# A layer-norm variance computed from its parts and a tile list cut in two, in a single-core attention and mixture-of-experts kernel

## The reference

```python
x = x + _layernorm(attention_block(_layernorm(x), ...))      # heads, two inner layer norms, a small feed-forward
x_flat = _layernorm(x).reshape(-1, 128)                      # 4096 rows
router_probs = softmax(x_flat @ gate_w)                      # 8 experts
expert_idx, expert_w = argmax and its probability
for e in range(8):
    y = gelu(x_flat @ w1[e] + b1[e], approximate=False) @ w2[e] + b2[e]     # 128 -> 512 -> 128
    out = out + where(expert_idx == e, expert_w, 0)[:, None] * y
x = x + _layernorm(out)
```

## Time and profile before

| what | value |
|---|---|
| median of 3 runs | 532.84 us (529.25, 532.84, 534.83) |
| the profiled execution's own time | 529.64 us |
| its span | 527.8 us |
| busy PE / DVE / ACT / POOL | 371.3 / 401.3 / 352.7 / 260.5 us |
| mean granted TensorE clock | 0.875 of 2.4 GHz |

### The profile page before, as it was taken

How to read it: one execution, slowest core, us unless ns; L and a number is a source line. 1 busy time by engine, 2 the same in 40 slices (tenths; PEclk the granted TensorE clock), 3 DMA queues, 4 the chain that set the end, 5 groups by cost and what they waited for, 6 DMA issues and landing times.

```text
span 527.8 us, 8507 instructions
## 1 busy us (share of the span) xinstructions
PE 371.3 (70%) x2412; PEld 255.7 (48%) x2412; DVE 401.3 (76%) x877; ACT 352.7 (67%) x730; POOL 260.5 (49%) x399
## 2 busy tenths in 40 slices
PE   0858688887777878887787889773000499999960
PEld 0744356554444444544444433663000388888840
DVE  4987658899999999999999973588783037667670
ACT  0234434888988888889888794788440387777730
POOL 8365015544444445545333103673667027777774
PEclk9999956788999899889999889976555699999995
DMA  9561211455555465545545199990111217776600
GB/s 208 41 145 36 57 31 41 103 141 126 129 141 133 110 140 121 126 115 141 143 121 127 38 125 151 132 239 21 42 36 57 74 51 193 217 194 177 172 15 0
DMA packets 81244, 58.18 MB, mean 110 GB/s; under 512 B 17619, under 2 KB 72919, under 8 KB 81196
## 3 DMA queue, kind: packets, MB, share of 16 engines
q1 hardware_dynamic: 75142, 53.12, 45.6%
q0 software_dynamic: 2496, 4.29, 2.4%
q10 hardware_dynamic: 3558, 0.20, 0.5%
HBM read 35.38 MB, written 23.11 MB: 111 GB/s over the span
## 4 chain that ended last, share of the span: by engine, by line
DVE 35%; PE 33%; POOL 8%; issue 8%; ACT 7%; DMA 6%; ACTq 1%; SPq 1%; POOLq 0%; DVEq 0%
DVE mxs L1753 10%; DVE big L1802 7%; PE ps L1593 7%; DVE big L1837 7%; PE ps L1604 6%; POOL sorted_rows L783 4%; DVE gb L1667 2%; PE ps L1265 2%; DMA qk_parts<-proj 2%; PE ps L1223 1%; PE ps L1537 1%; DMA arena<-m_parts 1%; PE ps L1396 1%; PE ps L1383 1%; PE ps L1538 1%
## 5 line engine op out<-in xcount | busy, mean ns | idle before, releaser
L1837 DVE SCALAR_TENSOR_TENSOR big<-big,ps 128x1024 f32<-128x1024 f32 x64 | 76.6, 1214 | 7.1 <-PE ps L1396 6.7
L1753 DVE TENSOR_REDUCE mxs<-ps 128x4 f32<-128x1024 f32 x64 | 76.6, 1217 | 2.4 <-PE ps L1265 1.2
L1802 DVE SCALAR_TENSOR_TENSOR big<-big,ps 128x1024 f32<-128x1024 f32 x64 | 74.5, 1215 | 4.0 <-ACT big L916 3.9
L925 ACT ACTIVATE big<-big 128x1024 f32<-128x1024 f32 x64 | 66.1, 1052 | 8.3 <-DVE big L1837 8.1
L916 ACT ACTIVATE big<-ps 128x1024 f32<-128x1024 f32 x64 | 63.5, 1016 | 10.5 <-PE ps L1383 10.1
L1383 PE MATMUL ps<-proj 128*128 128x256 f16 x256 | 43.4, 305 | 23.8 <-DVE mxs L1753 15.1
L695 POOL CAST mtok<-mxs 128x8 bf16<-128x8 f32 x32 | 6.1, 191 | 105.0 <-DVE mxs L1753 105.0
L808 POOL DMA_INDIRECT out_dram<-arena,fidx x46 | 46.9, 1019 | 17.5 <-issue 17.2
L2176 DVE TENSOR_SCALAR arena<-ps,x_all 128x128 f32<-128x128 f32 x46 | 14.0, 347 | 51.3 <-PE ps L1613 51.1
L1396 PE MATMUL ps<-arena 98*128 98x256 bf16 x256 | 42.5, 294 | 7.0 <-DVE big L1802 5.0
L1143 ACT ACTIVATE x_all<-x_all 128x128 f32<-128x128 f32 x46 | 20.1, 488 | 40.5 <-DMA x_all<-sorted_rows 40.5
(11 more groups left out here) (353 smaller groups left out, 889.0 us busy)
## 6 DMA issues: line engine op xcount, KB each, us to landing
big<-in_L_ffn_w_dram SPq DMA_DIRECT2D x46, 256.0 KB, 3.1
qk_parts<-proj SPq DMA_DIRECT2D x16, 384.0 KB, 2.9
arena<-qk_parts SPq DMA_DIRECT2D x32, 192.0 KB, 3.4
sorted_rows<-zrow SPq DMA_DIRECT2D x16, 266.0 KB, 3.7
arena<-qk_parts SPq DMA_DIRECT2D x32, 128.0 KB, 3.9
proj<-u_parts SPq DMA_DIRECT2D x48, 64.0 KB
x_all<-sorted_rows SPq DMA_DIRECT2D x23, 133.0 KB, 2.7
sorted_rows<-zrow SPq DMA_DIRECT2D x2, 1263.5 KB, 25.0
```

What stands on the lines that cost most here:

```text
L925: nc.scalar.activation(W[par1][:, n, :], W[par1][:, n, :], ACT.Exp).then_inc(p_ready, 1)
L1753: nc.vector.tensor_reduce(mxs[:, b1 % 2, :, 2 * n:2 * n + 2], src, AX_X, ALU.max, negate=True).then_inc(unit_free, 1)
L1802: nc.vector.scalar_tensor_tensor(W[par][:, n, :], W[par][:, n, :], 10.0, f, ALU.add, ALU.mult).then_inc(unit_free, 1)
L1837: nc.vector.scalar_tensor_tensor(W[par][:, n, :], W[par][:, n, :], 0.05, slot_of("log", b, n), ALU.mult, ALU.add).then_inc(unit_free, 1)
```

## The change

1. Half 1's third variance is computed by parts as well. `times_x` and `dot_x` run for all 8 groups (GpSimd does groups 4 to 6 ahead of its first transfer and group 7 behind the fourth), `square_x` and `var_x` go, groups 6 and 7 are scaled by ScalarE like the others, and `newton(6)`, `weight_in(1)`, `places(1)` and `weight_out(1)` stand ahead of the sums of rows 12 and on (`add_x(3)` and those of groups 4 to 7).
2. The tile list comes in two parts. Once 20 transfers' rows are counted (`TF` = 20), `first_tiles` lists three tiles that are full already (`NF` = 3: 2560 rows less 8 times 255 leave more than 512), and the others come from `other_tiles`. No tile is fixed any more: SyncE reads three numbers, loads three tiles' weights, waits for 20 transfers (`scat_first`) and loads their rows; then the same for tiles 3 to 5 with the rest of the list and the other 12 transfers. TensorE and ScalarE run the three tiles in an order of their own, and ScalarE loads the Gelu table ahead.

```diff
 (sizes)
+    TF = TH + GT
+    NF = -(-(TF * P - NE * (TS - 1)) // TS)
 (sync)
-            for j in range(DEPTH):
-                weights_in(j, slice(j, j + 1))
-            sp.wait_ge(scat, 16 * NT)
-            for j in range(DEPTH):
-                blk = RB * (j // 2) + (RB - 1) * (j % 2)
-                rows_in(j, slice(blk, blk + 1))
             sp.wait_ge(rsem["x"], 1)
+            no = [tile_no(j) for j in range(NF)]
+            for j in range(NF):
+                weights_in(j, bass.ds(no[j][0], 1))
+            sp.wait_ge(scat_first, 16 * TF)
+            for j in range(NF):
+                rows_in(j, bass.ds(no[j][1], 1))
+            sp.wait_ge(rsem["x"], 2)
+            no = [tile_no(j) for j in range(NF, DEPTH)]
+            for j in range(NF, DEPTH):
+                weights_in(j, bass.ds(no[j - NF][0], 1))
+            sp.wait_ge(scat, 16 * (NT - TF))
+            for j in range(NF, DEPTH):
+                rows_in(j, bass.ds(no[j - NF][1], 1))
 (gpsimd)
             def times_x(g):
                 pool.wait_ge(step["t"], g + 1)
-                nc.gpsimd.tensor_tensor(tx[g], t_of(g), x_all[...], ALU.mult).then_inc(step["tx"], 1)
+                if g >= GH:
+                    pool.wait_ge(step["dot"], g - GH + 1)
+                nc.gpsimd.tensor_tensor(tx[g % GH], t_of(g), x_all[...], ALU.mult).then_inc(step["tx"], 1)
...
+            for g in range(GH, NG - 1):
+                times_x(g)
             pool.wait_ge(z_stored, 16 * (NB + 4))
-            scatter(0, 0, TH)
+            scatter(0, 0, GT)
+            times_x(NG - 1)
+            scatter(0, GT, TH)
             scatter(1, 0, TH)
 (scalar)
             root(2)
             square_t(7)
             scale_c(1)
+            scale_b(2)
             root(4)
-            scale_b(2)
-            scale_b(4)
             scale_c(2)
-            scale_b(5)
             scale_b(3)
-            scale_c(3)
-            for g in range(GH, NG):
-                square_x(g)
             root(6)
             table(2, ACT.Exp)
+            scale_c(3)
             exps(1)
+            for g in range(GH, NG):
+                scale_b(g)
...
+            table(3, ACT.Gelu)
+            f_xr(0, 0); f_xr(0, 1); f_xT(0, 0); f_xT(0, 1); f_xr(0, 2)
+            act.wait_ge(fs["bias"], 1)
+            f_gelu(0, 0); f_xT(0, 2); f_yT(0, 0); f_gelu(0, 1); f_yT(0, 1); f_gelu(0, 2)
+            f_xr(0, 3); f_xr(0, 4); f_xT(0, 3); f_yT(0, 2); f_xT(0, 4); f_xr(0, 5)
+            act.wait_ge(fs["bias"], 2)
+            f_loop(act, f_body, NF)
 (tensor)
+            f_in(0, 0); f_in(0, 1); f_up(0, 0); f_up(0, 1); f_in(0, 2); f_down(0, 0); f_up(0, 2)
+            f_back(0, 0); f_down(0, 1); f_back(0, 1); f_down(0, 2); f_in(0, 3); f_up(0, 3); f_in(0, 4)
+            f_loop(pe, f_body, NF)
 (vector)
             weight_out(0)
+            dot_x(4)
             weigh(7)
             var_z(1)
+            dot_x(5)
             newton(2, step["rb"])
-            add_shift(6)
             var_o(1)
             gate_o(1)
             add_x(1)
-            add_shift(7)
+            add_shift(2)
+            dot_x(6)
             newton(4, step["rc"])
+            dot_x(7)
+            dots(1)
+            var_by_parts(1)
             logits(1)
+            add_shift(3)
             best(1)
-            add_shift(2); add_shift(4)
+            newton(6, step["rd"])
             add_x(2)
-            add_shift(5); add_shift(3)
+            weight_in(1)
+            places(1)
+            weight_out(1)
             add_x(3)
             for g in range(GH, NG):
+                if g == GH + 2:
+                    first_tiles()
+                add_shift(g)
                 add_x(g)
-            places(1); var_x(1); newton(6, step["rd"]); weight_in(1); weight_out(1)
-            (list of 15 further tiles, biases of 23)
+            other_tiles()
+            bias_of_first()
+            bias_of(NF, NS)
```

More of the change, by code:

```diff
@@ L254, in bass_sandwich @@
         REST = NS - DEPTH * (ROUNDS - 1)
-        assert DEPTH <= NE and REST >= 4
+        assert DEPTH <= NE and REST >= 4 and NF == 3 and NF + 3 <= DEPTH
         fbias = sb("fbias", [P, NS, EC + 1])
@@ L339, in bass_sandwich, with f_loop @@
         g_cos = gb[:, 0:2, :, :].rearrange("p a t n -> p (a t n)")
-        def f_loop(eng, body):
-            for j in range(DEPTH):
+        def f_loop(eng, body, first=0):
+            for j in range(first, DEPTH):
                 body(0, j)
@@ L1170, in _ @@
             f_xT(0, 0)
+            f_xT(0, 1)
             f_xr(0, 2)
-            f_xT(0, 1)
             act.wait_ge(fs["bias"], 1)
-            f_loop(act, f_body)
+            f_gelu(0, 0)
+            f_xT(0, 2)
+            f_yT(0, 0)
+            f_gelu(0, 1)
+            f_yT(0, 1)
+            f_gelu(0, 2)
+            f_xr(0, 3)
+            f_xr(0, 4)
+            f_xT(0, 3)
+            f_yT(0, 2)
+            f_xT(0, 4)
+            f_xr(0, 5)
+            act.wait_ge(fs["bias"], 2)
+            f_loop(act, f_body, NF)
         @block.tensor
@@ new lines, in dots @@
+            def dots(h):
+                of_h = slice(h * TH, (h + 1) * TH)
+                dve.wait_ge(step["dot"], GH * (h + 1))
+                chain(nc.vector.tensor_tensor(T(18, h), T(17, h), T(3, h), ALU.mult))
+                chain(nc.vector.tensor_tensor(T(18, h), d2[:, of_h], T(18, h), ALU.add))
+                chain(nc.vector.tensor_scalar(T(12, h), T(4, h), -LN_EPS, None, ALU.add))
+                chain(nc.vector.tensor_tensor(T(19, h), std0[:, of_h], std0[:, of_h], ALU.mult))
@@ L2019, in best, with var_by_parts @@
+            def var_by_parts(h):
+                dve.wait_ge(step["rc"], h + 1)
+                chain(nc.vector.tensor_tensor(T(12, h), T(12, h), T(5, h), ALU.mult))
+                chain(nc.vector.scalar_tensor_tensor(T(12, h), T(18, h), 2.0 / C, T(12, h), ALU.mult, ALU.add))
+                chain(nc.vector.tensor_tensor(T(12, h), T(12, h), T(5, h), ALU.mult))
+                nc.vector.tensor_tensor(T(6, h), T(12, h), T(19, h), ALU.add).then_inc(step["vd"], 1)
             def best(h):
@@ new lines, in first_tiles @@
+            def first_tiles():
+                rows_to(flat(4, 1).rearrange("p (e t) -> p e t", t=TH)[:, :, TF - TH - 1])
+                chain(nc.vector.tensor_scalar(til, cnt, 1.0 / TS, -(TS - 1) / (2.0 * TS), ALU.mult, ALU.add))
+                chain(nc.vector.tensor_scalar(til, til, MAGIC, None, ALU.add))
+                chain(nc.vector.tensor_scalar(til, til, -MAGIC, None, ALU.add))
+                chain(nc.vector.tensor_tensor_scan(end, ones[:, 0:NE], til, 0.0, ALU.mult, ALU.add))
+                chain(nc.vector.tensor_tensor(beg, end, til, ALU.subtract))
+                nc.vector.tensor_scalar(end, end, float(NF), None, ALU.min)
+                chain(nc.vector.tensor_scalar(beg, beg, float(NF), None, ALU.min))
+                nc.vector.tensor_scalar(at, beg, -1.0, None, ALU.mult)
+                chain(nc.vector.tensor_tensor(taken, end, beg, ALU.subtract))
+                tiles(0, NF)
@@ new lines, in other_tiles @@
+            def other_tiles():
+                rows_to(last_row(NH - 1))
+                chain(nc.vector.tensor_scalar(til, cnt, 1.0 / TS, (TS - 1) / (2.0 * TS), ALU.mult, ALU.add))
+                chain(nc.vector.tensor_scalar(til, til, MAGIC, None, ALU.add))
+                chain(nc.vector.scalar_tensor_tensor(til, til, -MAGIC, taken, ALU.add, ALU.subtract))
+                chain(nc.vector.tensor_tensor_scan(end, ones[:, 0:NE], til, 0.0, ALU.mult, ALU.add))
+                chain(nc.vector.tensor_tensor(beg, end, til, ALU.subtract))
+                chain(nc.vector.tensor_tensor(at, taken, beg, ALU.subtract))
+                tiles(NF, NS)
@@ new lines, in bias_of @@
+            def bias_of(s0, s1):
+                n = s1 - s0
+                for e in range(NE):
+                    to = fpart if e else fbias
+                    by = te[:, s0:s1, e:e + 1]
+                    nc.vector.tensor_tensor(to[:, s0:s1, 0:EC], eb1_sb[:, e:e + 1, :].to_broadcast([P, n, EC]),
+                                            by.to_broadcast([P, n, EC]), ALU.mult)
+                    chain(nc.vector.tensor_tensor(to[:, s0:s1, EC:EC + 1], eb2_sb[:, e:e + 1].unsqueeze(1).to_broadcast([P, n, 1]), by, ALU.mult))
+                    if e:
+                        chain(nc.vector.tensor_tensor(fbias[:, s0:s1, :], fbias[:, s0:s1, :], fpart[:, s0:s1, :], ALU.add))
+                nc.vector.sem_inc(fs["bias"], 1)
@@ L2088, in _ @@
             dot_x(3)
-            dots()
-            var_by_parts()
+            dots(0)
+            var_by_parts(0)
             add_shift(0)
@@ L2117, in _ @@
             add_x(3)
             for g in range(GH, NG):
+                if g == GH + 2:
+                    first_tiles()
+                add_shift(g)
                 add_x(g)
-            places(1)
-            var_x(1)
-            newton(6, step["rd"])
-            weight_in(1)
-            weight_out(1)
```

(3 more changed lines are left out.)

161 lines of the change are left out of this document (69 added, 92 removed).

## The result

The changed kernel takes 535.39 us (median of 20 runs, 530.80 to 540.96), the kernel before 531.71 us beside it (20 runs, 525.90 to 538.60). The ratio is 1.0094, with a 95% interval from 1.0067 to 1.0121: **0.9% slower**, where I had forecast 2% faster. The profiled execution took 534.64 us with a span of 532.8; that of before 529.64 with 527.8. So 5.0 us of span are to be explained.

A forecast was written before the change was run, and what follows sets the result against it. TensorE idles over 40 us before the experts, waiting on GpSimd's 32 transfers. Part 1 about nothing, part 2's early tiles gain 9.0: 529.64 - 9.0 = 520.6, put at 522 as the runs' median lies higher; range 515.5 to 530.

The forecast's parts named there:

- the measure: Expert stage: end of the fourth tile's second block, 436.2 us before, forecast 427.2; its shift is the shift of the end.
- rival C: GpSimd's transfers stretch beside VectorE's work; with twelve stretched, plus 7.8 us, 537.4 us in all; chance 0.05.
- What hides the rest: Second list near 399.5, its numbers and weight issues by 406.5, hidden under transfers ending at 411.4; biases by 406.
- The restart: Pipeline from third to fourth tile: scaling, transposes, copies and blocks, 9.6 us from ScalarE's start on tile 4 at 417.6.
- the three tiles took: TensorE from first rows to the end of the third tile's second block: +16.2 us, ending at 418.1.
- transfer 20: Last transfer the first three tiles wait for: ends 396.1, counted at 397.5, before the rows' issue at 398.3, so not late.
- the rule of the Trainium skill: GpSimd and a two-SBUF-input VectorE instruction exclude each other throughout; three variance products would cost up to 3.5 us.
- my row: VectorE instruction 0.29 us alone, 1.17 beside a GpSimd product; taken as 1.0 a product, 3.0 for three, first transfer 366.0.
- Rival A: Transfers end last, not the three tiles; fourth tile waits for the last transfer: gain 11.6 us, 518.0 us; chance 0.20.
- Rival B: TensorE's clock stays at half speed through the three early tiles: 5.5 us less, gain 3.5, 526.1 us; chance 0.12.
- Rival D: Nothing gained: VectorE reaches the first list later than counted, each us of delay losing one; 527 to 530 us; chance 0.15.

The follow-up runs named there:

- the kernel without bounds: Changed kernel, number loads without min/max bounds, one instruction instead of three: ratio to the kernel before 0.9842; again on another chip 518.53 us, ratio 0.9860.
- the gate by three: Changed kernel, each GpSimd transfer waiting for the arrival of the third before it: ratio to the kernel before 1.0109; with number loads without bounds 525.71 us, 0.9912.
- the gated kernel: Changed kernel, each transfer waiting for the last but one, at most two under way: 530.41 us, ratio to the kernel before 1.0023; again 531.50 us, 1.0005.

## Why the prediction was wrong

**The step that failed** is in part 2: "SyncE now reads numbers before it can ask for any weights ... Three tiles: 3.9 ... Six weight issues at 0.46 end at 398.3." The 1.31 us of a tile's two loads and the 0.46 of an issue come from the expert stage or from weights asked for ahead of the transfers; nothing in the trace of before shows SyncE executing while half 1's transfers run, because it executed nothing between 350 and 412. I priced 33 instructions at 6.7 us, by a row from another stage, and gave them no bound from the other side. They took 23.1 us, and the rows were asked for 16.2 us late (414.47 for 398.3). They then landed in 2.17 us instead of the 3.6 I had counted, 14.7 us late (416.64 for 401.9); the third tile's end was 15.3 us late (433.4 for 418.1) and the measure 14.05 (441.25 for 427.2). A forecast gain of 9.0 became a loss of 5.05. None of my rivals had it; rival C looked for the transfers to suffer from the engines, and it was the engines that suffered from the transfers.

**What hides the rest** was wrong with it: the second numbers and weights, "by 406.5, under transfers that end at 411.4", came at 416.0 to 423.2, behind the transfers and not under them. That cost nothing in this trace: the chain from the third tile to the fourth runs through ScalarE's Gelu and its own next piece (430.90 to 433.98), not through a wait for rows.

**The rest held**, and can be checked against a run in which SyncE kept its speed. In the second profile of the kernel without bounds the first transfer starts at 362.24 and the measure is 421.90 + 1.89 = 423.79: 61.6 us. The forecast had 427.2 - 366.0 = 61.2, the kernel before 436.2 - 363.04 = 73.2. The restart, from the third tile's second block to the fourth's, took 423.79 - 415.94 = 7.9 us (7.8 in the changed kernel); my working had 9.1 (its eight pieces add up to 9.5 us from ScalarE's start on tile 4, where it wrote 9.6). That the totals agree to 0.4 us is in part luck: the rows landed 0.8 us later than counted from the first transfer (398.91 - 362.24 = 36.7 for 35.9), the three tiles took 17.0 us for 16.2, and the shorter restart, 1.2, gave most of that back. This run also has no bounds, so that its numbers took 2.2 us (387.14 to 389.38) and not my 3.9. The span of 515.4 is 12.4 below before, 11.6 of it from the first transfer on. One term was off even there: transfer 20, "not late" by my count, took 4.69 us from its start to its arrival beside the weights, and it, not SyncE, held the rows until 395.56.

```profile
390.68 4.69 DMA sorted_rows<-proj,sl_i
```

**Part 1**, "about nothing, with bounds from -4 to +3": ratio 0.9998 alone, and in the changed kernel the first and last transfer within 0.5 us of forecast. Right. Three of VectorE's instructions beside the products took 1.15 to 1.66 us where the like take 0.2 to 0.7 alone, one of them an addition:

```profile
358.45 1.66 DVE L2014 TENSOR_TENSOR u_sb<-u_sb,be2c_bc 128x512 f32<-128x512 f32 x1
```

By the rule of the Trainium skill ("SBUF — State Buffer", section "Who interferes with whom") the first transfer would have started at 366.5 (an estimate: 3.5 us for three products instead of 3.0), by my row at 366.0; it was 366.33, between the two, so this trace agrees with the rule and doesn't tell it from my row.

**Rival A** (the transfers end last) fell: they ended 3.5 us before SyncE asked for the first rows. **Rival B** (the clock) fell: after a first pair of blocks in 5.59 us the next took 1.89. **Rival C**: one transfer of 1.45 us, none over 2. **Rival D** put the delay on VectorE before the list; the list came 0.4 us early.

That the stream of transfers slows the other engines is shown by three things: the slow pace appears beside it in the kernel before as well, it ends 2.5 to 3.6 us after GpSimd's last transfer instruction in all eleven slow profiles, and holding the transfers back removed it on both chips where that could be seen. What inside the chip is shared no run shows, nor why one chip shows no slow step at all. The changed kernel itself was never run on that chip; going by the run without bounds it might have gained there.

## What to carry to other kernels

A duration taken from one stage is a price for that stage. Before work is moved to an engine that was idle, look at what runs beside it there, and measure a few unused instructions at that very place in the old kernel (long enough: six loads missed what twenty showed). Where SyncE has to work beside a stream of GpSimd's indirect transfers, count its instructions, not its DMAs: bounds on a number load are two of its three instructions, and where the slow pace was, dropping them was worth about 2% (1.0109 to 0.9912 with the gate by three on one chip), where it was not, 0.2% at most (1.0010 to 0.9986, within the noise). The lowest time found, 518.53 us, has no bounds and comes from the chip without slow steps, so it is not the price of the bounds. And take the control on the same chip as the change: one profile that escapes elsewhere says nothing about the edit it happens to carry.

## What the runs showed of the hardware

- Beside half 1's transfers (steps of 1.27 us) SyncE went in steps of 0.70 us, 33 instructions in 23.1 us (60 in 19.3 in the kernel before), and ScalarE and SyncE took turns at that rate when both had work. SyncE and ScalarE fell into it 1 to 3 us after they took up work there, VectorE 6.5 us later than SyncE, and not at all in 10.8 us of work while SyncE was idle; it ended 2.5 to 3.6 us after the last transfer's instruction. GpSimd's own pace did not change. With at most two transfers under way it was absent in both profiles from chips that had it otherwise, with three or four it was there (23.1 and 23.3 us from list to rows).
- The slow steps came on some chips and not on others: none in four profiles of four kernels on one chip, gated or not, and in all profiles with bounds from the other chips (up to 0.71 us for a move of 0.03 us, in the expert stage too).
- A transfer of 0.96 us of GpSimd's time arrived 3.5 to 5 us after its start while 1.57 MB of weights were being loaded, about 2.3 us otherwise. The chain of the gated kernel:

```profile
389.43 2.36 DMA sorted_rows<-proj,sl_i
...
399.34 4.76 DMA sorted_rows<-proj,sl_i
```

- TensorE's clock fell where the early tiles left a longer pause. In the gated kernel it idled 5.77 us between the third and the fourth tile, and the next two first blocks took 3.75 us each instead of 1.97; windows of that stretch and of the steady stage (the last figures are the granted clock, the DMA share, GB/s) have it at 0.50, the lower of its two levels (1.2 of 2.4 GHz), and at 1.00:

```profile
427.70:431.40 3.70, 3.70 (x9) 2.88 (x10) 0.00 (x0) 0.20 (x1) 0.00 (x0) 0.50 0.76 229
441.00:445.00 4.00, 4.00 (x22) 3.54 (x22) 2.65 (x13) 3.18 (x8) 2.93 (x5) 1.00 0.67 186
```
